# A decoder layer on one core: when the context tile is clipped and rounded, and where the output weights, a shift row and the quantised context are loaded

## The reference

```
q, k, v = heads(x @ qkvw + qkvb)
probs   = softmax(q @ k.T / sqrt(32))
x = layernorm(x + (probs @ v) @ ow + ob)
fq(a, s, z) = (clip(round(a / s + z), 0, 255) - z) * s
x = layernorm(x + fq(x) @ fq(ctx))                # ctx: 2 x 1024 x 1024
x = layernorm(x + x @ W_base.T + b_base + two of 8 low-rank experts(x))
```

## Time and profile before

| | |
|---|---|
| median of 3 runs | 710.16 us (709.98 to 711.01) |
| profiled execution | 711.73 us, of which the span of instructions is 709.9 us |
| TensorE (PE) busy | 98% of the span |
| DVE, ScalarE (ACT), GpSimd busy | 66%, 59%, 41% |
| granted TensorE clock, mean | 0.998 |
| DMA queue of SP | 98.36 MB, 45.2% of the 16 engines |

### The profile page before, as it was taken

How to read it: one execution, slowest core, us unless ns; L and a number is a source line. 1 busy time by engine, 2 the same in 40 slices (tenths; PEclk the granted TensorE clock), 3 DMA queues, 4 the chain that set the end, 5 groups by cost and what they waited for, 6 DMA issues and landing times.

```text
span 709.9 us, 11767 instructions
## 1 busy us (share of the span) xinstructions
PE 694.6 (98%) x3489; PEld 527.0 (74%) x3496; DVE 468.7 (66%) x833; ACT 416.8 (59%) x807; POOL 289.4 (41%) x209
## 2 busy tenths in 40 slices
PE   6999999999999999999999999999999999999996
PEld 5777778777787787787777877866767777888885
DVE  6887466575585575665755756567688679785574
ACT  5458577685685685776856856864567672221111
POOL 6692180171162153134126149836644734131130
PEclk9999999999999999999999999999999999999999
DMA  8656436346345444543643475755824332131101
GB/s 288 190 173 218 128 79 205 86 120 198 89 119 154 131 119 131 157 116 97 193 117 87 122 231 149 234 186 187 279 96 166 120 119 90 60 148 59 60 30 60
DMA packets 55956, 99.20 MB, mean 140 GB/s; under 512 B 11008, under 2 KB 21632, under 8 KB 55024
## 3 DMA queue, kind: packets, MB, share of 16 engines
q1 hardware_dynamic: 55632, 98.36, 45.2%
q10 hardware_dynamic: 288, 0.39, 0.2%
HBM read 56.41 MB, written 16.65 MB: 103 GB/s over the span
## 4 chain that ended last, share of the span: by engine, by line
PE 90%; issue 3%; SPq 3%; DMA 2%; DVE 2%; ACT 0%; POOL 0%; POOLq 0%; DVEq 0%
PE bank L482 57%; PE st_pair L612 8%; PE bank L626 8%; PE bank L582 7%; SPq L265 2%; PE bank L733 2%; PE st_pair L733 2%; PE st_pair L759 2%; PE st_pair L482 2%; PE bank L535 1%; DMA c_raw<-in_ctx 1%; DMA qp<-m_row 1%; PE bank L748 1%; PE bank L718 1%; DMA big_raw<-in_xT 0%
## 5 line engine op out<-in xcount | busy, mean ns | idle before, releaser
L1446 DVE TENSOR_REDUCE columns<-bank 128x1 f32<-128x512 f32 x256 | 172.9, 687 | 77.7 <-PE bank L582 77.2
L904 ACT ACTIVATE bank<-bank,columns 128x512 f32<-128x512 f32 x256 | 169.2, 661 | 31.2 <-DVE columns L1446 29.3
L899 ACT ACTIVATE probs<-st_pair 128x1024 f32<-128x1024 f32 x112 | 114.9, 1025 | 95.0 <-PE st_pair L612 94.2
L482 PE MATMUL bank<-big_hi,w_hi 128*128 128x512 f32 x368 | 146.0, 397 | 6.1 <-DVE big_lo L1338 6.1
L482 PE MATMUL bank<-big_hi,w_lo 128*128 128x512 f32 x368 | 144.2, 392 | 0.0
L482 PE MATMUL bank<-big_lo,w_hi 128*128 128x512 f32 x368 | 144.2, 392 | 0.0
L582 PE MATMUL bank<-kp,qp 128*128 128x512 f32 (+1 forms) x256 | 100.6, 393 | 1.6 <-ACT bank L904 1.5
L612 PE MATMUL st_pair<-qp,kp 128*128 128x512 f32 x256 | 86.1, 392 | 0.5 <-ACT probs L899 0.4
L1175 POOL TENSOR_SCALAR c_raw<-c_raw,sc 128x1024 f32<-128x1024 f32 x16 | 19.2, 1202 | 164.0 <-DMA c_raw<-in_ctx 160.3
L482 PEld LDWEIGHTS bank<-big_hi,w_hi 128*128 128x128 f32 x368 | 69.7, 189 | 20.1 <-DVE big_lo L1338 6.1
L482 PEld LDWEIGHTS bank<-big_hi,w_lo 128*128 128x128 f32 x368 | 69.6, 189 | 14.9
(11 more groups left out here) (183 smaller groups left out, 1128.0 us busy)
## 6 DMA issues: line engine op xcount, KB each, us to landing
w_raw<-in_wqkv SPq DMA_DIRECT2D x7, 1536.0 KB, 9.0
c_raw<-in_ctx SPq DMA_DIRECT2D x16, 512.0 KB, 4.0
qp<-q_hi SPq DMA_DIRECT2D x128, 64.0 KB
kp<-k_hi SPq DMA_DIRECT2D x124, 64.0 KB
big_raw<-in_xT SPq DMA_DIRECT2D x16, 256.0 KB, 5.6
qp<-q_lo SPq DMA_DIRECT2D x64, 64.0 KB
c_scratch<-c_q SPq DMA_DIRECT2D x16, 256.0 KB, 2.2
r_all<-r_scratch SPq DMA_DIRECT2D x64, 64.0 KB, 2.0
```

The costliest lines, as they stand in the source:

```text
L482: mm = nc.tensor.matmul(dst, lhs[a], rhs[b], start=(k == 0 and n == 0) if first is None else False, stop=(k == last_k and n == 2))
L899: nc.scalar.activation(probs[:, j, t:t + 2, :].rearrange("p t q -> p (t q)"), st_pair[:, :], ACT.Exp).then_inc(sem["exp_ok"], 2)
L904: nc.scalar.activation(bank(max_bank(s, n)), bank(max_bank(s, n)), ACT.Exp, bias=m_col[:, n:n + 1], accum_out=l_col[:, 1 - par, n:n + 1]). ...
L1446: nc.vector.reduce_max(m_col[:, n:n + 1], bank(max_bank(s, n)), AX, negate=True).then_inc(sem["rowmax"], 1)
```

## The change

It moves instructions and adds or removes none. On DVE, rounding goes from after n = 13 to the end of the step (behind `copy_recip`) in steps 2 to 14; in step 2 the clip goes there too. Steps 0, 1 and 15 keep their places. On SP, `load_ow` goes behind the last packing in steps 14 and 15; behind step 15, `store_shift(16)` goes ahead of a wait for the transposed scores and `load_residual(0)`, and the load of the first half of the quantised context (`load_c2(0)`, 2 MB) goes from ahead of both to behind `spread_recip(15)`.

```diff
@@ SP, step @@
                 if maxima:
                     store_shift(s, par)
-                if isinstance(s, int) and s >= UNITS - 2:
-                    load_ow(s + 2 - UNITS, 3 * s + 3)
                 if proj:
                     pack(s, par, 2, "k")
                     if 3 not in early:
                         pack(s, par, 3, "q")
                     pack(s, par, 3, "k")
+                if isinstance(s, int) and s >= UNITS - 2:
+                    load_ow(s + 2 - UNITS, 3 * s + 3)
+                if proj:
                     if begin:
                         load_w()
@@ SP, behind step 15 @@
             load_tile(2)
             load_tile(3)
-            load_c2(0)
+            store_shift(UNITS, 0)
             sp.wait_ge(sem["st_mm"], NS * (UNITS - 1))
             load_residual(0)
-            store_shift(UNITS, 0)
-
-
             store_recip(UNITS - 1)
             spread_recip(UNITS - 1)
+            load_c2(0)
             load_residual(1)
             store_context(UNITS - 1, 1, G - 1)
@@ DVE, step @@
-                    if proj and n == 8 and not begin and not second:
+                    if proj and n == 8 and not begin and not early:
                         clip_context(s)
...
-                    if proj and n == 13 and not begin and not second:
+                    if n == 13 and isinstance(s, int) and s == UNITS - 1:
                         round_context(s)
...
                 if maxima and proj:
                     copy_recip(s - 1)
+                if isinstance(s, int) and s == 2:
+                    clip_context(s)
+                if proj and not begin and not second and not (isinstance(s, int) and s == UNITS - 1):
+                    round_context(s)
```

## The result

The changed kernel took 717.23 us (median of 5, 716.83 to 717.92), the kernel before 711.01 us in the same comparison (5 runs, 709.98 to 711.58). The ratio is 1.0093 (95% interval 1.008 to 1.0106): 6.6 us slower. That is the forecast direction, but the forecast was 714.2 and its range ended at 717.0. The profiled execution took 717.66 us with a span of 715.9; the granted clock fell from 0.998 to 0.994, and the mean of each of the five executions is 0.994 or 0.996.

A forecast was written before the change was run, and what follows sets the result against it. The prediction took TensorE, busy 98% of the span, as the bound. From the profiled 711.73 us, minus 2.4 gains, plus 4.5 (step 15) and 2.0 (step 16), gave 715.8; less 1.57, a median of 714.2 us, range 711.3 to 717.0.

The forecast's parts named there:

- The chain from the late weights to S12: Step 15: late weights delay GpSimd's splits and scaling, then DVE's clip and maxima; TensorE loses 4.3 us with restart.
- the 4.5 of the sum: Step 15's whole cost: 4.3 us of TensorE stall plus 0.2 for the shifted rounding.
- rival C: Clock falls in step 15's stall; matmuls behind it run at half speed, 2.4 us more, 716.6 us; chance 0.17.
- Step 16: The late second half of the output weights stalls TensorE in step 16 by 2.0 us (bounds 0 and 2.8).
- The gains: Step 2's clip 1.7, rounding at the step's end 0.4, shift rows ahead of the 2 MB load 0.3: 2.4 us.
- clip of step 2 at the end: In step 2, DVE's maxima no longer queue behind a clip awaiting the late context tile; gain 1.7 us.
- The rounding's term of 0.4 us: Rounding at the end of steps 2 to 14 avoids GpSimd's two-input subtraction in step 5; gain 0.4 us.
- The base: Starting time of the forecast: the kernel before at a median of 710.16 us, its profiled execution at 711.73.
- A: Rival: the late weights are covered in step 15, only the gains remain, 707.8 us; chance 0.09.
- B: Rival: only step 15 stalls, step 16's 2.0 us fall away, 712.2 us; chance 0.17.
- D: Rival: the tail stalls too, by 1.5 us, from the later second x tile, 715.7 us; chance 0.08.

The follow-up runs named there:

- ow_early: The changed kernel with load_ow back ahead of the last packs, everything else of the change kept; 708.9 us, ratio 0.9977 to the kernel before.
- clip15_end: The changed kernel with clip and rounding of step 15 also at the end of the step, weights still late; 715.75 us, ratio 1.0059 to before.
- the two kernels between: The changed kernel with load_ow among the ten packs: ahead of the last three (713.82 us), or behind the first three (709.88 us).
- filler: The changed kernel with 16 unused 512-column matmuls added in step 15 ahead of S12; 716.75 us, ratio 1.008 to before.
- half1_late: The changed kernel with step 14's load_ow back ahead of the last packs, only step 15's behind them; 712.37 us, ratio 1.0019 to before.
- ow_behind_q3: The changed kernel with load_ow ahead of the last three of the ten packs; 713.82 us, ratio 1.0041 to before.
- tail_alone: The kernel before with only the change's SP edits behind step 15 (shift rows first, 2 MB context load later); 710.27 us, ratio 0.9994.
- ow_late_alone: The kernel before with only load_ow moved behind the last packs; 720.93 us, ratio 1.0131 to before.
- dve_alone: The kernel before with only the change's VectorE edits (rounding of steps 2 to 14 and clip of step 2 at the end); 709.51 us, ratio 0.9987.

## Why the prediction was wrong, step by step

*The chain from the late weights to S12* was right in each link. The weights' first split began 5.5 us after the load's issue (5.4 assumed), the clip stood idle 6.01 us (5.9), S12 was held up 4.6 us at the full clock's pace (4.3 with the restart). The chain was confirmed by ow_early, clip15_end and the two kernels between. In filler, where the clock stays up, step 15 is 32.6 us long against 28.1 before: 4.5 more, the 4.5 of the sum.

*The step that failed* is that the sum ran the matmuls behind the stall of step 15 at the full clock and put nothing for the lower level; that was left to rival C, at 0.17. By the mean clocks it fell in every timed execution of the changed kernel. For 4.3 us of matmuls behind S12 the array ran at 1.2 GHz, which is 2.1 us, and step 15 became 6.7 us longer than before where 4.5 had been put. The rows for it were there: the clock had fallen 2.5 us before the end of the span, within 4 us of the last matmul, and the stall that I predicted was longer. I weighed step 2's stall of 1.0 us against it, which says nothing on one of 4. The Trainium skill (TensorE: Matmul & The Clock Gate, HAM oscillation) says that a wait between two groups of matmuls can put the array back to the lower clock. The trace agrees: 4.63 us idle, and 0.51 behind it.

*Step 16* took 2.2 us more than before (2.0 predicted), and that agreement is luck. At the full clock, which the forecast assumed, it takes 3.0 more (filler; 2.9 in half1_late): the term was 1.0 too small. The sum had the second half 5.7 us late against TensorE. GpSimd's first split of it, in the changed kernel and in filler:

```profile
455.49 0.62 POOL L1156 TENSOR_SCALAR big_hi<-big_raw 128x512 fp32r<-128x512 f32 x1 [8.57 <-DMA big_raw<-in_ow]
...
454.56 0.62 POOL L1160 TENSOR_SCALAR big_hi<-big_raw 128x512 fp32r<-128x512 f32 x1 [7.21 <-DMA big_raw<-in_ow]
```

Step 16 opens at 441.80 and 440.07, so the splits begin 13.69 and 14.49 us into it; before, where step 16 opened at 437.70, it was 445.84 - 437.70 = 8.14. The second half is 5.5 us late in the changed kernel and 6.3 in filler. S12 came 25.9 and 25.7 us into step 15, so it is the slow matmuls behind it that brought TensorE later to step 16 and gave this cover back.

*What each is worth in the total.* The sum gave +4.1 us (4.5 + 2.0 - 2.4) and +6.6 was measured. Filler, at the full clock, has +5.7: step 16 has 1.0 and the gains 0.8 of the difference. The clock adds 0.9 net, which the noise does not tell from nothing. So the lower level is shown in the trace, with its 2.1 us in step 15; how much of it reaches the end is open.

*The gains* were sized 2.4 and measured 1.6 (ow_early). The term "clip of step 2 at the end", 1.7 us, was read from an execution in which a load took 6.7 us; in most it takes 5.5 to 5.8 and hides. Even with the slow load it is not all gained, as step 3's first transposed score shows in ow_early and ow_behind_q3, whose load took 6.8 and 6.9 us:

```profile
78.58 0.74 PE L610 MATMUL st_pair<-qp,kp 128*128 128x512 f32 x2 [0.24 <-DMA qp<-m_row]
...
78.64 0.74 PE L611 MATMUL st_pair<-qp,kp 128*128 128x512 f32 x2 [0.52 <-DMA qp<-m_row]
```

TensorE comes to step 3 about 2.2 us earlier than before, but SP issues the shift rows at 76.1 as before (76.28), so TensorE waits for them. Step 3 takes 28.5 and 28.7 us there, 28.1 in the changed kernel's first profile, and 27.9 in all seven that have the rounding at the end and the fast load. Why SP stands late in those executions stays open.

The rounding's term of 0.4 us was rather too small. Steps 3 to 14 take 334.5 to 334.8 us in those seven profiles, and 335.2, 335.1 and 336.9 in the three with the rounding between the maxima (before, tail_alone, ow_late_alone): 0.4 to 2.2 us lost, in steps 3 and 5 above all. With this and now and then the clip of step 2, the 0.9 of dve_alone can be understood; its split over steps is not measured.

*The base.* The forecast started from 710.16; the five runs beside the changed kernel gave 711.01, and later comparisons 710.3 to 710.7. The 0.85 lifts C's 716.6 to 717.4, out of the range; without it, 710.16 x 1.0093 = 716.8 would have lain just inside.

*Rivals.* A was refuted by the 8.2 us between ow_early and the changed kernel, B by step 16's 2.2 us, D by tail_alone. C's mechanism is what happened. Its time, 716.6, is 0.6 below the measured one, but it is added up with gains 0.8 too large and with a step 16 that is right only by the luck told above.

## What to carry to other kernels

When a load moves down a queue, follow what waits for it through the in-order engines: here it was not the user of the weights that stalled TensorE in step 15, but a scaling queued behind their split, and then maxima queued behind a clip. When a sum yields an idle time of TensorE of several us, look up in the trace how soon after idling the granted clock has fallen there, and add the matmuls behind the stall at the lower level as a term, not as a rival. Then ask what the next stall gives back: here a later TensorE found step 16's weights less late. And before a stall in one profile is booked as a gain, ask whether its cause is a DMA whose time varies: one execution cannot tell.

## What the runs showed of the hardware

In the profiles the granted clock fell in idle times of 4.6 us (changed), 4.4 (ow_late_alone) and 0.87 + 3.15 with one matmul between (clip15_end), and not in 2.38 us (ow_behind_q3) or in 0.81 behind a filled wait (filler). The 2.38 is one execution: in 8 of 12 of that kernel the mean clock was 0.992 to 0.996, under all executions of the kernel before (0.997 or more). The lower level lasted 6.8 or 3.4 us in these profiles, and the part of it in which TensorE had work cost that work half its speed.

A DVE tensor_scalar from SBUF to SBUF took 0.73 us alone and up to 2.78 when it started 0.17 us behind a two-input GpSimd instruction of 2.40: it ended 0.55 us after that one, as if it had waited for it whole. The rounding of the earlier trace rows started 1.26 us behind such an instruction, took 1.68 and ended 0.55 us after it too.

The same load of one context tile took 5.5 to 5.8 us in nine profiles and 6.7 to 6.9 in four.
